# Layer 0's edge pass: the 8 relation columns move into the fetch ring, and each tile is multiplied once

## What is computed

```python
h = jnp.maximum(_layernorm(x, axis=-1), 0.0)
# layer 0: nfeat = h, efeat = edge_attr_128
agg  = segment_sum((h * norm_src[:, None])[src], dst)      # 128 columns
conv = agg @ W * norm_dst[:, None] + b
esum = segment_sum(efeat @ We + be, dst)                    # kernel: sum efeat first, 128 columns
out  = conv + (h @ W + b) / (in_deg + 1) + esum / clip(in_deg, 1)
# in_deg, and per relation cnt[dst, edge_type] of layer 2: counts of edges, 8 columns
```

## Time and profile before

| | |
|---|---|
| median of 3 runs | 8363.43 us (8358.21 to 8364.93) |
| the profiled execution | 8344.47 us, of it span 8342.7 us |
| layer 0's edge pass | 218 to 1522 us of the span, 1304 us, 832 tiles |
| layer 2's second pass (`l2f`), same function | 5266 to 6477 us, 832 tiles |
| busy over the span | PE 58%, PEld 44%, DVE 47%, ACT 12%, POOL 50% |
| granted TensorE clock, mean of the span | 0.65 (0.57 in layer 0's pass) |

### The profile page before, as it was taken

One profiled execution on the slowest core, in us unless ns is written; L12 is line 12 of the kernel. 1 busy time (PEld: TensorE's weight loads), 2 busy tenths in 40 slices (PEclk: granted clock), 3 DMA queues, 4 the chain that ended last, 5 costly groups with the idle time before them and its releaser, 6 DMA issues. The chain is left out here.

```text
span 8342.7 us, 101911 instructions
## 1 busy us (share of the span) xinstructions
PE 4833.0 (58%) x22262; PEld 3709.0 (44%) x22262; DVE 3900.6 (47%) x11420; ACT 1003.5 (12%) x3034; POOL 4161.7 (50%) x4338
## 2 busy tenths in 40 slices
PE   4778778645555555559566666433333455555556
PEld 4666667534444444324344444333333244444445
DVE  7444444634444445324555555333333344444445
ACT  4000000411111111125000000000000311111113
POOL 1566666255545544100666666566666354554552
PEclk9655555756666666579787887555555656666667
DMA  2433333233223323105444444211112322232333
GB/s 54 119 84 84 84 85 84 72 95 90 90 87 89 91 87 77 50 0 239 141 132 133 127 133 123 56 45 45 45 45 44 108 89 87 88 90 88 89 91 78
DMA packets 409987, 738.67 MB, mean 89 GB/s; under 512 B 96778, under 2 KB 263523, under 8 KB 402772
## 3 DMA queue, kind: packets, MB, share of 16 engines
q0 software_dynamic: 173824, 438.05, 19.7%
q1 hardware_dynamic: 227188, 289.28, 10.4%
q10 hardware_dynamic: 8592, 6.82, 0.3%
HBM read 614.99 MB, written 120.01 MB: 88 GB/s over the span
## 5 line engine op out<-in xcount | busy, mean ns | idle before, releaser
L1198 POOL DMA_INDIRECT xh<-pair_d,src_i x1664 | 1646.4, 989 | 1566.3 <-DVE l3te_ve L1507 559.1
L1895 POOL DMA_INDIRECT l2e_rows<-msg_d,msg_i x832 | 801.0, 963 | 959.5 <-POOLq L2126 505.1
L722 PE MATMUL l0e_ps<-l0e_rows,l0e_sel 128*128 128x256 f32 x1664 | 949.7, 673 | 303.9 <-DVE l0e_sel L742 252.2
L689 POOL DMA_INDIRECT l0e_rows<-node_d,src_i x832 | 788.0, 947 | 511.0 <-issue 219.0
L689 POOL DMA_INDIRECT l2f_rows<-msg_d,msg_i x832 | 789.1, 948 | 444.0 <-issue 230.3
L722 PE MATMUL l2f_ps<-l2f_rows,l2f_sel 128*128 128x128 f32 x1664 | 431.0, 439 | 786.7 <-DVE xh L756 519.8
L1988 PE MATMUL l2e_ps<-l2e_rows,l2e_sel 128*128 128x256 f32 x1664 | 554.9, 485 | 417.8 <-DVE l2e_sel L2077 402.3
L722 PEld LDWEIGHTS l2f_ps<-l2f_rows,l2f_sel 128*128 128x128 f32 x1664 | 371.3, 327 | 846.9 <-issue 444.7
L756 DVE TENSOR_TENSOR early_acc<-early_acc,l0e_ps 128x264 f32 x832 | 357.3, 429 | 657.6 <-PE l0e_ps L724 268.5
L1988 PEld LDWEIGHTS l2e_ps<-l2e_rows,l2e_sel 128*128 128x128 f32 x1664 | 390.3, 245 | 572.7 <-DVE l2e_sel L2077 445.8
L724 PEld LDWEIGHTS l0e_ps<-l0e_of_rel,l0e_sel 128*128 128x128 f32 x1664 | 532.9, 320 | 138.3
(11 more groups left out here) (435 smaller groups left out, 7980.5 us busy)
## 6 DMA issues: line engine op xcount, KB each, us to landing
l0e_rows<-in_edge_attr_dram SPq DMA_DIRECT2D x832, 64.0 KB
msg_d<-l2a_msg SPq DMA_DIRECT2D x50, 1024.0 KB, 3.8
l1te_local<-local_d SPq DMA_DIRECT2D x52, 512.0 KB
xh<-pair_d,src_i POOLq DMA_INDIRECT x1664
l2e_local<-local_d SPq DMA_DIRECT2D x52, 512.0 KB
l3te_local<-local_d SPq DMA_DIRECT2D x52, 512.0 KB
msg_d<-l2e_msg SPq DMA_DIRECT2D x50, 512.0 KB
l0e_rows<-node_d,src_i POOLq DMA_INDIRECT x832
```

Source lines behind the costliest of these rows:

```text
L689: pool.indirect_dma_start(rows[:, t % R, 0:width], None, table, bass.IndirectOffsetOnAxis(index[:, t:t + 1], 0)).then_inc(gathered[t % R], 16)
L722: mm = nc.tensor.matmul(ps[b][s][:, 0:full], sel[:, b, s, :], rows[:, r, :], start=True, stop=True)
L1198: pool.indirect_dma_start(rows[:, t % R, :], None, g.pair_d, bass.IndirectOffsetOnAxis(g.src_i[:, t:t + 1], 0)).then_inc(gathered[n % RG], 16)
L1895: pool.indirect_dma_start(rows[:, t % R, :], None, table, bass.IndirectOffsetOnAxis(index[:, t:t + 1], 0)).then_inc(gathered[t % R], 16)
```

## The change

The 8 indicator columns get a place in the ring `rows` itself, whose slots become 264 columns wide for layer 0 (1056 bytes instead of 1024). DVE writes them there with one instruction per group of four tiles, at the same point of its program and after the same waits as it wrote `of_rel` before; the tile `of_rel` is gone. PE multiplies `sel` once with all 264 columns. `gather_sum` for layer 2 (`attr` is None) keeps its width.

```diff
-        rows = st.sb("rows", [P, R, full])
+        wide = full + RELS if attr is not None else full
+        rows = st.sb("rows", [P, R, wide])
-        of_rel = st.sb("of_rel", [P, 2, G, RELS])
...
-                        mm = nc.tensor.matmul(ps[b][s][:, 0:full], sel[:, b, s, :], rows[:, r, :], start=True, stop=True)
-                        if attr is not None:
-                            mm = nc.tensor.matmul(ps[b][s][:, full:full + RELS], sel[:, b, s, :], of_rel[:, b, s, :],
-                                                  start=True, stop=True)
-                        mm.then_inc(summed, 1)
+                        nc.tensor.matmul(ps[b][s][:, 0:wide], sel[:, b, s, :], rows[:, r, :],
+                                         start=True, stop=True).then_inc(summed, 1)
...
-                def make_sel_and_add(t0, b, first=False, adds=True):
+                def make_sel_and_add(t0, q, first=False, adds=True):
+                    b = q % 2
...
-                            of_rel[:, b, :, :], g.rel[:, bass.ds(t0, G)].unsqueeze(2).broadcast_to([P, G, RELS]),
+                            rows[:, q * G:(q + 1) * G, full:wide], g.rel[:, bass.ds(t0, G)].unsqueeze(2).broadcast_to([P, G, RELS]),
```

More of the change, by code:

```diff
@@ L758, in _ @@
                 for q in range(R // G):
-                    make_sel_and_add(q * G, q % 2, first=q < 2, adds=q > 0)
+                    make_sel_and_add(q * G, q, first=q < 2, adds=q > 0)
                     if attr is not None and q == 1:
@@ L763, in _ @@
                     for q in range(R // G):
-                        make_sel_and_add(R * i + q * G, q % 2)
+                        make_sel_and_add(R * i + q * G, q)
                 ws = windows_of(nc, g, mybir.EngineType.DVE, T - G)
```

## The result

The kernel after takes 8495.80 us (median of 4 runs, 8483.84 to 8508.97) beside 8363.89 us before (median of 4, 8358.21 to 8364.93): ratio 1.0159, 95% interval 1.0142 to 1.0177. It is 132 us slower, where 70 us faster was forecast. The profiled execution took 8501.59 us, of it span 8499.8.

What follows compares the result with a forecast made beforehand. Neither PE (1.28 us per tile) nor POOL (1.25) alone explained 1.554; POOL was to set the pace next at 1.47. 832 x (1.554 - 1.47) = 70 us off 8363.4 gave 8293, range 8273 to 8330 (8 in 10: 8262 to 8380).

Steps and rivals of the forecast that it cites:

- PE, per tile ... I take 0.93: PE's tile in layer 0's pass without the 8-column product: 0.93 us, 0.35 us less, bounds 0.93 to 1.03 at the lower clock.
- The loop of PE and DVE ... 0.98 us per tile: PE waits about 0.2 us per group for DVE's `sel`, making 0.98 us per tile, still below POOL's 1.25.
- DVE ... I take none: DVE's indicator instruction, 193 ns per four tiles, writes four pieces instead of one: no difference, at most 0.06 us per tile.
- SP and the transfers ... I take nothing: Attribute transfers keep number and bytes, with slots starting 1056 bytes apart instead of 1024: no time added.
- POOL, which sets the pace next ... Eight issues and one wait: POOL's eight issues of 1.25 us plus one 1.78 us wait: 11.78 us, 1.47 us per tile in layer 0's pass.
- The wait of the second kind: POOL's wait of about 1.8 us after eight issues, from a stall of all engines together; claimed to stay.
- of the first kind: POOL's wait of about 1.8 us after four issues, for a tile PE has only just done; claimed to end.
- Rival 3: DVE and PE can't catch up 12 tiles between stalls: 1.62 us per tile, 52 us more, 8415; chance of slower 0.12.
- Against: POOL must wait earlier, after eight: Objection to Rival 3: if PE is behind, POOL waits after eight issues, which breaks the run and the stall.
- Rival 4: DVE's `sel` blocks POOL's issues, up to 0.28 us more per tile: 1.53, 20 us off, 8343; chance 0.04.
- The signs: Expected in the profile after: two PE records per tile, 70 to 104 long POOL waits, pace 1.45 to 1.50, idle before `sel`.
- a cycle of 12 tiles still takes 18.8 us: Layer 0's cycle keeping its length of 18.8 us, named as one of two outcomes that would prove the forecast wrong.

## Why the prediction was wrong

**"PE, per tile ... I take 0.93": near.** The records stand 0.44 us apart at the lower clock, 0.88 per tile, a little under the least of the bounds (the mean of 0.45 from `l2e` has the first step of a group, 0.57 us, in it), and 0.22 to 0.25 at the higher one (2.02 us for eight, the last one's tail with it). PE's busy time fell from 1021 to 693 us, more than the 0.35 us per tile make, since its clock was higher in the waiting (0.67 beside 0.57). The time went nowhere because PE didn't set the pace.

**"The loop of PE and DVE ... 0.98 us per tile": right that it lies below POOL's 1.25.** Without gathers it runs at 0.79, at a granted clock of 0.98; the 0.98 us were worked out at the lower clock, at which no run shows this loop alone.

**"DVE ... I take none" and POOL's issues: right.** 194 ns beside 193, and 947 beside 947.

**"SP and the transfers ... I take nothing": wrong.** PE's wait for attributes went from 26.2 to 326.7 us. The reason that I had named as a sign, the slots' new distance, is excluded by the slots of 1280 bytes (1.0156 beside 1.0159). The Trainium skill, DMA: Bandwidth & Descriptors, section How a descriptor splits into AXI transactions, says that a descriptor which doesn't start at a multiple of 256 bytes fetches bytes before its start that it doesn't use. The section tells of what is read, and the slots are what is written, so it speaks less plainly against the change than the prediction had it. The runs show no difference between slots 1056 and 1280 bytes apart, at a share of 0.28 for the transfer engines in the kernel after. The transfers were late because SP issued them late. I had looked at bytes, landings and the share of the transfer engines, and not at the time that SP's program needs per transfer inside a run of POOL: 12.92 us for four.

**"POOL, which sets the pace next ... Eight issues and one wait": the step that failed.** "The wait of the second kind stays, as PE doesn't cause it" is true, but its size was taken as fixed at 1.8 us, and the runs as remaining 8 long. PE's wait, "of the first kind", was what broke POOL's issues after four. With it gone the runs are 12 long, their wait 6 us, and the cycle is 15 + 5.7 = 20.7 us. The step's price was 1.47 us per tile and the measured one 1.73: 832 x 0.26 = 216 us between them, about the 209 us by which the pass missed its forecast (1443 beside 1234). What the step describes exists: it is the kernel with the rest every eight, 12.03 us per eight tiles, 1.504 per tile, 8297 us on a chip where before took 8342. The forecast named the right cycle for a kernel that nothing in the change produces, so the 8297 us of that kernel are no support for the forecast of 8293.

**Rival 3, "Slower", had the side and the place.** It said a cycle of 12 and 19.4 us, decided once POOL's wait passes 3.8 us; it is 20.7 and 6.0. It lacked SP; without SP's transfers the pace is still 1.68 us per tile. Its "Against: POOL must wait earlier, after eight" failed: in the about 6 us before DVE crawls, PE finishes eight tiles (the two groups of eight records from 1119.25 to 1125 us; median over the runs 8 at 6.25 us), so the wait ahead of the ninth issue is met when POOL comes to it. `l2f`, on whose 2.6 us I had relied, has no transfers on SP in its loop and shorter adds; its runs are of 12 too (65 of 67), and DVE has over 500 slow instructions in the pass. It showed the crawl, and not its price here.

**Rival 4** had the right pair of engines in the wrong direction: it is not DVE that holds up POOL's issues, whose mean stays at 944 to 951 ns in every kernel with all its gathers, but POOL's issues that go with slow instructions of DVE and SP.

**The signs.** Two records per tile, DVE 194, POOL 947: seen; the records stand 0.44 us apart, where 0.46 to 0.47 was named. POOL waits once per twelve issues, 69 times in the whole pass, at the edge of the 70 to 104 named, at about three times the length forecast. PE's idle time grew, but more of it ends with the attribute transfers (326.7 us) than with `sel` (110.1), where nearly all was to stand before `sel`. The pace was named as 1.45 to 1.50 and "a cycle of 12 tiles still takes 18.8 us" as what would prove me wrong; it took 20.7.

Shown by the runs: the shorter PE tile alone brings the loss (two products restore it, dropping the 8-column product in the old layout makes it); the runs of 12 end where PE's finished tiles fall short, at all three leads; the slow instructions need POOL's gathers, and runs longer than four with a rest between; a rest of 2.3 us every eight or a second queue turns the loss into a gain. Argued only: that the slow instructions are themselves what makes DVE and SP late. In the kernel before DVE has 3 of them and yet stands 2.3 us in its runs of eight.

Open: by what means POOL's issues slow the other engines' instructions; why with two queues part of the runs break after four. A long run is not enough for it. In `l2e` of the kernel before, whose gathers carry twice the bytes, 21 runs have 12 issues or more, and of DVE's 95 register instructions later than 5.7 us into them none is slow (loads of registers aren't in this count; 5 of those took 0.6 to 0.8 us in the whole pass). In layer 1's and layer 3's edge passes POOL issues 16 at a time, and none of DVE's 1759 register instructions is slow. In those three passes DVE's program has no branch; in the two passes where DVE crawls, `l0e` and `l2f`, it is a loop, and so is SP's. Whether a DVE and an SP without a loop would stay fast here, no run tried (PE's program in `l0e` is a loop too, and in the kernel after none of its register instructions is slow).

Also, the count of slow instructions is a sign and not a price: the kernel before with the rest every eight has 451 on SP, and its PE waits between 300 and 1450 us for an attribute transfer only once, 1.8 us.

The versions that beat both kernels clearly are the change with a second queue (8304.91, ratio to before 0.9935, 0.9914 to 0.9957), with a rest every eight (8296.70, 0.9941, 0.9924 to 0.9957) and with both (8211.89, 0.9943, 0.9913 to 0.9973). They are not to be told apart.

## What to carry to other kernels

Before an engine that is not the bound is made faster, ask whose queue its slowness was pacing: here PE's second product, which looked like pure waste, kept POOL's issues in bursts of four and eight, beside which DVE and SP kept up. When a sister loop is used for a forecast, compare its queues as well as its engines, since a queue that it lacks (SP's here) is the one that may be late. Where idle time ends with "issue" and grows with another engine's burst, look at how long the waiting engine's register instructions take, and try a rest in the burst: here it is two lines and worth more than the work that was removed. It has to be placed by trial: every eight issues it gained, every four it lost.

## What the runs showed of the hardware that was not expected

- Register, branch and transfer-issuing instructions of DVE and SP take 0.70 to 0.73 us instead of 0.03 to 0.06 (0.33 for an issue) in the kernel after, from 5.7 us (DVE) and 2.1 us (SP) after the start of a run of 12 of POOL's indirect transfers until about 2 us after its last one. Without such transfers there is no slow instruction between 300 us and the end of the pass at 879; with a rest after every four there is none either. In `l1te`, `l3te` and `l2e` of the kernel before, where DVE's program has no loop, none of DVE's register instructions is slow, beside runs of 12 to 16.
- Of two rests every eight, 2.3 us is enough and 1.1 us is not (128 beside 469 slow instructions on DVE, 1.504 beside 1.599 us per tile).
- A gather of 128 rows lands 2.45 us (median, rest every four) after its issue began, and a POOL that waits for it issues again 3.3 us after that beginning, behind runs of four and of eight alike.
- A second queue for the same transfers was worth 18 us on one kernel and 191 us on the other.
